# Queries' blocks written over all 128 partitions with a mask per head, and waits for tables and constants moved to their first reader

## What is computed

```python
# stage A: autocorrelation per channel: FFT over the 128 rows, top 9 delays, softmax, weighted sum of shifted context
corr = ifft(fft(q) * conj(fft(k))).real;  w, idx = top_k(corr, 9);  w = softmax(w)
# stage B: base matrix plus 8 experts of rank 16, the two best per row
out = x @ W_base.T + b_base + lora(top2(softmax(x @ W_router.T)))
# stage C: windowed attention. 8 heads of 16 channels, 1024 positions, window 16
q = Wq x + bq;  k = Wk cond + bk;  v = Wv cond + bv          # 128 channels x 1024
dots = einsum('bhdt,bhdtw->bhtw', q, k_win) * 16 ** -0.5
out = einsum('bhtw,bhdtw->bhdt', softmax(dots), v_win);  out = Wo out + bo
# stage D: 4 experts of rank 16, the two best per row
```

## Time and profile before

| | |
|---|---|
| median of three runs | 1871.96 us (1867.45 to 1872.3) |
| span of the profiled execution | 1867.4 us; the run of 1867.45 us is the one that agrees with it |
| PE, DVE, ACT, POOL busy | 1708.1, 1569.8, 1165.5, 905.9 us |
| mean granted clock of TensorE | 0.971 |
| length of one step in the middle | about 55 us |
| ACT, query blocks (L876) | 384 instructions, 268.8 us |
| POOL, query blocks (L1450) | 128 instructions, 132.8 us |

### The profile page before, as it was taken

The page is one execution under the profiler, slowest core; times in us unless marked ns, Lnnn a source line. Parts: engine busy times, 40 slices in busy tenths (PEclk is TensorE's granted clock), DMA queues, the critical chain, the costliest instruction groups (busy, mean ns, idle before and its releaser), DMA issues.

```text
span 1867.4 us, 48204 instructions
## 1 busy us (share of the span) xinstructions
PE 1708.1 (91%) x19296; PEld 1082.9 (58%) x19296; DVE 1569.8 (84%) x4726; ACT 1165.5 (62%) x1929; POOL 905.9 (49%) x870
## 2 busy tenths in 40 slices
PE   3689999999999999999999999999999999999975
PEld 2356566666556666556666655666665566665553
DVE  6778898888889888888888888988888888888853
ACT  5257666666666665765666676666666566667642
POOL 2445544455554545555455555444555545455432
PEclk8799999999999999999999999999999999999985
DMA  5133322333332233332223333223334322333220
GB/s 208 34 58 69 58 50 48 54 69 69 69 48 47 54 61 69 69 58 53 48 51 69 69 69 57 49 48 55 69 69 64 51 48 48 67 69 58 29 30 24
DMA packets 549359, 111.37 MB, mean 60 GB/s; under 512 B 531088, under 2 KB 531344, under 8 KB 548624
## 3 DMA queue, kind: packets, MB, share of 16 engines
q1 hardware_dynamic: 549136, 108.29, 30.7%
HBM read 57.94 MB, written 16.78 MB: 40 GB/s over the span
## 4 chain that ended last, share of the span: by engine, by line
PE 56%; DVE 19%; ACT 9%; POOL 8%; issue 6%; DMA 1%; SPq 0%; DVEq 0%; ACTq 0%; POOLq 0%
PE pb L601 18%; PE pc L674 8%; ACT q_diag L876 6%; POOL rest L1422 4%; PE pa L561 4%; POOL prob L1422 4%; PE pa L523 3%; PE pa L497 3%; PE pa L524 3%; PE pa L498 3%; PE pa L499 3%; ACT v_im L778 3%; PE pb L590 2%; DVE rows_c L1249 2%; DVE x_c L1141 2%
## 5 line engine op out<-in xcount | busy, mean ns | idle before, releaser
L601 PE MATMUL pb<-w_base_h,even_words 128*128 128x512 f16 x1024 | 324.8, 379 | 0.0
L1459 POOL TENSOR_TENSOR sc<-sc,sc_rec 128x512 f32<-128x512 f32 x128 | 134.1, 1048 | 294.6 <-DVE sc_rec L1236 294.6
L876 ACT ACTIVATE q_diag<-sc,par 32x512 f32<-32x512 f32 x384 | 268.8, 715 | 10.3 <-DVE sc L1149 3.1
L1429 POOL TENSOR_TENSOR p_hl<-sc,p_hl 128x512 f16<-128x512 f32 x128 | 164.3, 1283 | 208.0 <-ACT p_hl L778 208.0
L601 PE MATMUL pb<-w_base_l,even_words 128*128 128x512 f16 x512 | 193.9, 379 | 0.0
L488 PE MATMUL pa<-xn_a,tab 128*128 128x512 f32 x384 | 181.7, 610 | 4.6 <-ACT xn_a L778 4.6
L674 PEld LDWEIGHTS pc<-sc_t,v_diag 128*128 128x128 f16 x6144 | 170.1, 97 | 20.6 <-DVE sc_t L1243 6.0
L674 PE MATMUL pc<-sc_t,v_diag 128*128 128x32 f16 x6144 | 173.9, 177 | 5.6 <-DVE sc_t L1243 5.6
L652 PE MATMUL pc<-k_h,q_diag 128*128 128x32 f16 x2048 | 169.2, 177 | 0.0
L653 PE MATMUL pc<-k_l,q_diag 128*128 128x32 f16 x2048 | 168.5, 177 | 0.0
L654 PE MATMUL pc<-k_h,q_diag 128*128 128x32 f16 x2048 | 168.5, 177 | 0.0
(11 more groups left out here) (166 smaller groups left out, 4619.6 us busy)
## 6 DMA issues: line engine op xcount, KB each, us to landing
x_a<-in_x SPq DMA_DIRECT2D x32, 512.0 KB, 5.5
x_res<-in_ctx_in SPq DMA_DIRECT2D x32, 512.0 KB, 5.1
x_res<-in_x SPq DMA_DIRECT2D x32, 512.0 KB, 3.7
v_diag<-even_words SPq DMA_DIRECT2D x128, 128.0 KB, 4.9
v_diag<-p_hl SPq DMA_DIRECT2D x128, 128.0 KB, 4.9
out<-rows_c SPq DMA_DIRECT2D x32, 512.0 KB, 2.6
v_diag<-in_base_w SPq DMA_DIRECT2D x4, 1024.0 KB, 10.0
q_diag<-in_ra SPq DMA_DIRECT2D x1, 544.0 KB, 13.7
```

What stands on the lines that cost most here:

```text
L601: mm(pb[:, h, :], rows[:, cols], weights[:, j, h * HALF:(h + 1) * HALF], start=(j == 0 and m == 0), stop=False)
L876: nc.scalar.activation(q_diag[rows, blocks, col:col + QB], source, ACT.Copy, scale=par[rows, a:a + 1]).then_inc(qd_out.sem, 1)
L1429: g_.tensor_tensor(part[:, :, :, LO], sc[:, g % 2, :, :], part[:, :, :, HI], ALU.subtract)\
```

## The change

`b_query_blocks` goes by head and not by pair. One instruction writes the 16 columns of one head, for one half of the blocks, on all 128 partitions; its scale is `own[:, head]`, a new table of 128 x 8 that is 1 on the head's own 16 partitions and 0 on the others. So every element of `q_diag` is written each time. The memset of `q_diag` and the semaphore `qdiag_set` are gone. The number of instructions, their order by head and half, and the 512 elements per partition stay: ACT writes the heads 0 to 5, POOL 6 and 7.

```diff
-            def b_query_blocks(b, pair, a, half):
-                if pair == 0 and a == 0:
+            def b_query_blocks(b, head, half):
+                if head == 0:
                     act.wait_ge(ql_out.sem, ql_out.after(b))
-                    act.wait_ge(qdiag_set.sem, 1)
-                    if not first(b):
+                    if first(b):
+                        act.wait_ge(w_lo.sem, WEIGHTS_SPLIT)
+                        act.wait_ge(tab_in.sem, TABLES_IN)
+                    else:
                         act.wait_ge(mm_sc.sem, mm_sc.after(b - 1, 2 * half + 2))
-                rows = slice(32 * pair, 32 * pair + 32)
...
-                nc.scalar.activation(q_diag[rows, blocks, col:col + QB], source, ACT.Copy,
-                                     scale=par[rows, a:a + 1]).then_inc(qd_out.sem, 1)
+                nc.scalar.activation(q_diag[:, blocks, head * QB:(head + 1) * QB],
+                                     q_hl.rearrange("p (n t) -> p n t", t=QB)[:, blocks], ACT.Copy,
+                                     scale=own[:, head:head + 1]).then_inc(qd_out.sem, 1)
...
-                    b_query_blocks(i - 2, 1, 1, 0)
-                    b_query_blocks(i - 2, 2, 0, 0)
-                    b_query_blocks(i - 2, 1, 0, 0)
-                    b_query_blocks(i - 2, 0, 0, 1)
-                    b_query_blocks(i - 2, 0, 1, 1)
-                    b_query_blocks(i - 2, 1, 0, 1)
+                    b_query_blocks(i - 2, 3, 0)
+                    b_query_blocks(i - 2, 4, 0)
+                    b_query_blocks(i - 2, 2, 0)
+                    b_query_blocks(i - 2, 0, 1)
+                    b_query_blocks(i - 2, 1, 1)
+                    b_query_blocks(i - 2, 2, 1)
                 if live(0):
                     a_values(i)
```

On POOL the same is done, and its waits for its own instructions are taken out:

```diff
-                g_.tensor_tensor(q_diag[pool_rows, blocks, col:col + QB], ...
+                g_.tensor_tensor(q_diag[:, blocks, head * QB:(head + 1) * QB], ...
                                  ALU.mult).then_inc(qd_pool.sem, 1)
-                pool.wait_ge(qd_pool.sem, qd_pool.after(b, 2 * half + a + 1))
...
-                if first(i - 0):
-                    clear_queries()
-                if live(0):
-                    pool.wait_ge(bias_added.sem, bias_added.after(i))
-                if live(0):
-                    pool.wait_ge(ln_rs[1].sem, ln_rs[1].after(i))
...
-                if live(-1):
-                    pool.wait_ge(sum_w.sem, sum_w.after(i + 1, 2))
-                if live(-1):
-                    pool.wait_ge(sum_w.sem, sum_w.after(i + 1, 1))
-                if live(1):
-                    pool.wait_ge(ln_rs[3].sem, ln_rs[3].after(i - 1))
```

The waits for tables and constants ahead of steps 0 and 1 are gone on all engines and stand in the functions that read them first, for the first element only: `a_query`, `b_router` and `b_queries` on PE, `b_keys` and `b_query_blocks` on ACT, `b_keys` on DVE, `b_query_blocks` on POOL. On ACT:

```diff
             def b_keys(b):
+                if first(b):
+                    act.wait_ge(const_set.sem, CONSTS_SET)
+                    act.wait_ge(const_in.sem, CONSTS_IN)
...
             for i in range(-2, BATCH + 4):
-                if i == 1:
-                    act.wait_ge(tab_in.sem, TABLES_IN)
-                    act.wait_ge(const_set.sem, CONSTS_SET)
-                    act.wait_ge(const_in.sem, CONSTS_IN)
-                step(i, i % 2, during(i))
+                step(i, during(i))
```

More of the change, by code:

```diff
@@ L151, in build @@
         band_bf = sb("band_bf", [P, KEYS], BF16)
-        par = sb("par", [P, 2])
+        own = sb("own", [P, HEADS])
         w_base_h = sb("w_base_h", [P, KT, D], F16)
@@ L701, in c_delta, with step @@
                 last.then_inc(mm_ffn[1].sem, 1)
-            def step(i, odd, live):
+            def step(i, live):
                 if live(2):
@@ L820, in spread @@
                     act.wait_ge(pt_out.sem, pt_out.after(b))
-                nc.scalar.activation(place[:, :], rows[:, slot, :] if n == 2 else rows[:, :], ACT.Square, bias=ln_lead[n][:, :], scale=-D ** -0.5,
+                nc.scalar.activation(place[:, :], rows[:, b % 2, :] if n == 2 else rows[:, :], ACT.Square, bias=ln_lead[n][:, :], scale=-D ** -0.5,
                                      accum_out=mv[n][:, 1:2]).then_inc(ln_mv[n].sem, 1)
@@ L1152, in b_keys @@
             def b_keys(b):
+                if first(b):
+                    dve.wait_ge(const_in.sem, CONSTS_IN)
                 dve.wait_ge(kh_out.sem, kh_out.after(b))
@@ L1382, in _ @@
             for i in range(-2, BATCH + 4):
-                if i == 1:
-                    dve.wait_ge(const_in.sem, CONSTS_IN)
-                step(i, i % 2, during(i))
+                step(i, during(i))
         @block.gpsimd
@@ L1436, in a_normalise, with b_query_blocks @@
                     .then_inc(prob_out.sem, 1)
[L1438 to L1444, removed]
+            def b_query_blocks(b, head, half):
+                if head == HEADS - 2:
                     pool.wait_ge(ql_out.sem, ql_out.after(b))
-                    if not first(b):
+                    if first(b):
+                        pool.wait_ge(w_lo.sem, WEIGHTS_SPLIT)
+                        pool.wait_ge(tab_in.sem, TABLES_IN)
+                    else:
                         pool.wait_ge(mm_sc.sem, mm_sc.after(b - 1, 2 * half + 2))
-                col = (2 * POOL_PAIR + a) * QB
                 blocks = slice(half * NBLK // 2, (half + 1) * NBLK // 2)
-                g_.tensor_tensor(q_diag[pool_rows, blocks, col:col + QB],
-                                 q_hl[pool_rows, :].rearrange("p (n t) -> p n t", t=QB)[:, blocks],
-                                 par[pool_rows, a:a + 1].unsqueeze(2).to_broadcast([32, NBLK // 2, QB]),
+                g_.tensor_tensor(q_diag[:, blocks, head * QB:(head + 1) * QB],
+                                 q_hl.rearrange("p (n t) -> p n t", t=QB)[:, blocks],
+                                 own[:, head:head + 1].unsqueeze(2).to_broadcast([P, NBLK // 2, QB]),
                                  ALU.mult).then_inc(qd_pool.sem, 1)
-                pool.wait_ge(qd_pool.sem, qd_pool.after(b, 2 * half + a + 1))
             def c_normalise(b, g):
@@ L1465, in clear_values, with step @@
                 g_.memset(v_diag[:, :, :, :, :], 0.0).then_inc(vdiag_set.sem, 1)
-            def clear_queries():
-                pool.wait_ge(w_lo.sem, WEIGHTS_SPLIT)
-                g_.memset(q_diag[:, :, :], 0.0).then_inc(qdiag_set.sem, 1)
-            def step(i, odd, live):
+            def step(i, live):
                 if live(1):
-                    b_query_blocks(i - 1, 1, 1)
+                    b_query_blocks(i - 1, 7, 1)
                 if live(0):
```

116 lines of the change are left out of this document (54 added, 62 removed).

## The result

The kernel after takes 1846.36 us (median of four runs, 1845.73 to 1847.06), the kernel before beside it 1870.68 (four runs, 1867.45 to 1872.3). The ratio is 0.9873 with an interval of 0.9861 to 0.9886: 24.3 us less, or 1.3%. The direction and the mechanism were right; two terms of the sum were too small, the recurring one and the one of the waits at the start. One execution of the kernel before, beside e5 to e7, took 4685.92 us and is left out everywhere as slow.

What follows compares the result with a forecast made beforehand. It took ACT's queue of query blocks ahead of v_im to delay DVE, and DVE to delay PE, once a step. Gains of 16.5 + 0.8 + 1.1 = 18.4 us from 1871.96 gave about 1853.5 us, range 1847 to 1866.

Steps and rivals of the forecast that it cites:

- The recurring term: In each of 30 steps, ACT's v_im copy starts 0.55 us earlier, helping DVE and PE: 16.5 us less.
- The waits at the start: ACT's first v_re copy no longer waits for bias_base, the last constant: 1.1 us won, bounds 0 and 1.10.
- Distance between two blocks: ACT's query blocks, all starting at partition 0, follow at 0.63 us, not 0.74; six take 3.87 us for 4.32.
- Price of one block: One ACT query block on 128 partitions still takes 715 ns, as on 32; bounds 617 and 787.
- POOL: POOL's wider blocks and its nine removed waits hide in its idle time: price 0, at most 0.3 us a step.
- the clear: Removing POOL's one memset of `q_diag`, 6.94 us, is off the path since POOL then idles for DVE: 0.
- The rival of no gain: The shorter distance has another cause than start partition, or v_im waits for more; only the start gains: 1870.9 us, 13%.
- that of slower: ACT and POOL, now sharing partitions of `q_diag`, make ACT's blocks dearer: 13 us more, 1885 us, 5%.
- The rival of another wait: DVE's product with v_im is held by DVE's queue or PE; about 0.25 us a step kept: 1862.6 us, 12%.
- DVE can use it all: it idles for 0.55 there: At DVE's product with v_im, its 0.55 us of idle time absorbs the whole 0.55 us by which v_im is earlier.
- PE does not wait for: Behind v_re, ACT's exponential comes some 0.3 us earlier, which DVE wants for its sums but PE does not need.
- Last element: In the last element nine ACT blocks stand alone on the chain, 5.76 us for 6.41; 0.8 us less with both ends.

Runs made afterwards that it cites:

- e5: Kernel before with ACT's blocks all starting at partition 0 but covering 32, 64 or 96 partitions by pair; 1848.86 us, ratio 0.9885.
- e7: Kernel before, narrow blocks kept, with `a_values` one block earlier in ACT's order (five blocks ahead of v_im, not six); 1853.22 us, ratio 0.9908.
- e4: Kernel before with ACT's 32-partition blocks reordered so that fewer neighbours change pair; 1860.68 us, ratio 0.994.
- e2: Kernel before with only POOL's blocks widened to 128 partitions and its nine waits removed; 1870.33 us, ratio 0.9995.
- e8: Kernel after with the clear of `q_diag`, its semaphore and ACT's and POOL's waits for it put back; 1845.73 us, ratio 0.9876.
- e1: Kernel before with only ACT's blocks widened to 128 partitions by the new table; POOL, clear and all waits stay; 1849.84 us, ratio 0.9883.
- e6: Kernel after with `a_values` two blocks earlier in ACT's order; 1845.83 us, ratio 0.9866.
- e9: Kernel after with the waits for tables and constants put back at the start on all engines; 1849.18 us, ratio 0.9895.
- e10: Kernel after, unchanged, run once more; 1846.43 us, ratio 0.9878.
- e3: Kernel before with only the waits for tables and constants moved to each engine's first reader; 1869.34 us, ratio 0.9989.

## What held of the prediction, and which of its terms were mis-sized

**What held.** *Distance between two blocks*: that ACT holds an instruction with another start partition was read from the earlier trace rows; e4 shows it by order alone and e5 rules the width out. *Price of one block*: 715 ns forecast, 710 measured. *POOL* and *the clear*: priced at 0, and e2 and e8 show 0. The rival of no gain fell with e1, that of slower with e1 and the groups by shape: 710 and 1044 ns with ACT and POOL on the same partitions. The rival of another wait was right in its place and not in its price: DVE's queue is the next limit (e6), but only behind the whole 0.64 us.

**The recurring term: 0.55 us a step forecast, 0.64 measured, 2.7 us of the miss.** It failed in two numbers of that step, both in the start of v_im and of the product. First, the distance of 0.63 came from the one repeated pair in the earlier trace rows, which stands behind a held block; between blocks that nothing holds it is 0.61, so six gain 0.54 instead of 0.45. Second, "DVE can use it all: it idles for 0.55 there" read the idle time as what could be won at most. But back to back DVE starts an instruction before the one in front ends: L1226 to L1059 is 0.60 for a duration of 0.69. In the timeline of before the same two stood 1.24 apart (1111.65 and 1112.89), so 0.64 could be won, and was. That "PE does not wait for" the earlier exponential held: e7 shows a price only when it comes later than before. The upper bound of the term, 0.61, was built from the same two readings and too low, and with the start's upper bound of 1.1 this made the low end of the range too high.

**Last element: 0.8 us forecast.** Nine blocks take 5.61 us (timeline of ACT in after) instead of the 5.76 forecast and the 6.41 of the earlier trace rows; with 0.1 ahead and 0.1 behind, 1.0 us. No run shows this term by itself.

**The waits at the start: 1.1 us forecast, 2.7 measured on the average of the profiles and 2.75 between e9 and e10.** The upper bound was DVE's idle time in one execution, and in that execution bias_base landed nearly as early as it ever did here. e3, with an interval of 0.4 to 3.6, agrees with both numbers. The profiles of before and after alone, 1.1 us apart at the first block, would have confirmed the wrong size: the step that failed is to have taken what one execution shows for the price of a wait whose length varies from execution to execution.

**The base.** The prediction took the profiled execution for the run of 1867.45. The runs now show the device time 1.8 us above the span (1846.75 and 1845.0), so the profiled one belongs to some 1869.2 us, and the median of before was 1869.18 to 1870.94 here, 1 to 3 us below the 1871.96 from which the forecast was taken.

**The new sum**: 30 x 0.64 = 19.2, last element 1.0, start 2.7: 22.9, beside 24.3, 22.8 (e10) measured. By parts e1 21.0, e2 0.5 and e3 1.5 are 23.0. What is left, about 1 us, is within the spread of before's runs, and a term that the prediction does not have can be that large: the granted clock in the tail. The three profiles in which ACT's blocks stand as in before have tails of 107.2 us (e2, clock 0.73), 108.5 (before, 0.69) and 109.8 (e3, 0.70); of the seven in which all of them start at partition 0, six take 105.7 to 105.8 at 0.76 to 0.78, and e9 106.6 at 0.71. So the tail varies by 2.5 us with the same blocks, and before and e9, at nearly one clock, differ by 1.9. Why the clock differs between executions stays open.

## What to carry to other kernels

When the same engine runs many short instructions behind each other, read their start-to-start distance in narrow windows, not their mean duration: here 0.13 us for each change of the start partition, on instructions of 710 ns, was nearly all of 21 us, and writing four times the data from one start partition was the faster way; where that isn't possible, an order with fewer changes brought 10 us (e4). What the next engine can gain at most is its start-to-start distance less the one that it has back to back (1.24 less 0.60 here), not its idle time in the profile (0.55). And a wait for the last transfer of a burst can't be priced from one execution: it was 2.7 us on average, and 1.1 in the pair of profiles at hand.

## What the runs showed of the hardware

- ACT holds an instruction whose start partition differs from the one before it until that has ended (0.74 us from start to start for blocks of 715 ns), and overlaps the others by 0.10 us (0.61), at 128 partitions (after) and at widths of 32, 64 and 96 mixed (e5). Another start of the input alone or of the output alone is enough (v_im and v_re in after). The rule that the Trainium skill, "VectorE: DVE Perf Modes", section "Two Vector instructions with no wait between them", has for VectorE thus holds for ScalarE in all cases seen here, with starts at 0, 32 and 64.
- An instruction right behind a held one starts at 0.63 us, not 0.61, in before and in e4. Why isn't known.
- ACT at 710 ns and POOL at 1044 on the same 128 partitions of one tile, partly at the same time, show no sign of contention (715 and 1037 on separate strips in before).
- In e7's profile one step takes 57.24 us for 54.44. The granted clock is at the lower of its levels (1.2 for 2.4 GHz) for 6.8 us of it, from 930.6 on; the 603 matmuls of the step are busy 55.7 us for 52.6, and all of the delay arises in these 6.8 us. Ahead of them PE idled 0.5 us at 927.8 and 0.7 at 929.7.
